# One launch for attention and routed experts: the opening drawn into the attention pipeline, and the output projection in plain fp32

## The chip, the cores and the metric

The kernel runs on one core of one Trainium2 chip. The metric is the device time of one execution in microseconds (us), as the median of several runs. The profile shown below is one further execution, taken by the hardware profiler.

## The reference, cut to what matters

```python
B, T, C = 4, 1024, 256          # 16 heads of 64; 32 experts, hidden 1024, 8 tokens for each expert
xn = layernorm(x)
# attention: causal, with rotary embedding
q, k, v = xn @ Wq, xn @ Wk, xn @ Wv                    # (B, T, 1024) each
q, k = rope(q), rope(k)
attn = softmax(where(causal, q @ k.T * 64**-0.5, -inf))
a = (attn @ v) @ Wo + bo
# experts: each expert picks its 8 tokens by a softmax over the tokens
probs = softmax(xn @ gate_w.T + gate_b, axis=tokens)
vals, idx = top_k(probs, 8)                            # for each batch and expert
merged = einsum(xn[idx], vals)                         # (B, 32, 256)
o = concat(gelu(concat(merged, 1) @ w1), 1) @ w2       # (B, 32, 256)
f = zeros.at[idx].add(o * vals)
out = x + a + f
```

All inputs and outputs are fp32.

## The kernel before

There are three blocks, one after the other, each with its own instruction lists for the five engines and a common barrier at its end (`build`).

`prepare_block` runs over the four batches: it loads x, normalises it (`normalise`), transposes it on TensorE, splits the transposed rows into a high half (rounded to fp32r) and a low half (the remainder), stores both in `xt_s`, and adds up the gate logits, 12 matmuls for each batch (L267). `route_block` makes the softmax over the tokens, picks the eight largest, stores the gates (`wsp_s`), merges the tokens of each expert (L379), splits Wo into halves and stores it (`wo_s`), and loads the rotation tables.

`attend_block` is a pipeline written out by hand. Its unit is a *pair*: two heads of one batch, 32 pairs in all (N = B x PAIRS), and a pair P has six *stages* (P, g), g = 0 to 5. The list STAGES gives the order in which every engine goes through its work, so an engine that has to wait holds back everything behind it in its list. In a stage, TensorE makes the scores of two chunks (`scores`, L1076 to L1088), the scores that give row maxima for the next pair (`maximum`, L1100 and L1106), one projection of a later pair (`fill`, L1130 for v, L1144 for q and k), and the products with v (`values`, L1169). ScalarE takes the exponentials (L818) and empties the projections (`evict`, L834 and L839), VectorE makes the maxima (L940), the rotation's first product and the low halves (L974, L964), GpSimd the rotation's second product and the sums of the exponentials, and SyncE issues most DMAs: the swapped rows of the rotation (`t_swap<-t_raw`, L743), the round trips through DRAM that spread the softmax sums (`store_sums`, `spread_recip`), and weights. For pairs below 8 the raw weights are loaded, split into halves (`weights_of`, L915 and L1049) and stored; later pairs load the halves.

Two kinds of work are hung into stages. *Slots* (`slots_of`) are the expert layers: for each of eight groups of four experts, four `layer1`, four `turn` and four `layer2` slots, in pairs -1 to 7; w1 and w2 (1 MB for each expert and layer) are loaded by ScalarE's queue. *Outputs* (`outputs_of`) are the 32 tiles of 128 rows of the result. A tile of batch y is computed in the first two pairs of batch y + 1; those of batch 3 stand behind the last pair. For each tile ScalarE rounds the attention's rows (`round_out`, L882), VectorE makes the remainder (`rest`, L1008), TensorE adds 24 matmuls with the three products of halves (L1218) and one fp32 matmul for the experts' part (L1221), and VectorE adds x and the bias (L1017). The product of the halves is this:

```python
for k in range(PAIRS):
    for o, hw in ((oh, 0), (oh, 1), (ol, 0)):
        pe.matmul(bank, o[:, t % 2, k, :], wo[:, hw, k, :], start=(a == 0), stop=False)
        a += 1
pe.wait_ge(moe_loaded, (y + 1) * 80)
pe.matmul(bank, wsp[:, t * P128:(t + 1) * P128], oe[:, :], start=False, stop=True)
```

The stages (-2, 0) to (-1, 5) fill the pipeline: projections of pairs 0 and 1, maxima of pair 0, and the first layer1 slots.

## Time and profile before

| | us |
|---|---|
| median of 3 runs (lowest, highest) | 1481.48 (1481.37, 1485.4) |
| the profiled execution, its own time | 1488.41 |
| span of the profile, first to last instruction | 1486.6 |
| granted TensorE clock, mean share over the span | 0.976 |

The span is cut below into stretches that start and end at the first exponential of a pair (L818): pair 0's is at 128.0 us, pair 1's at 176.9, pair 4's at 336.3, pair 5's at 384.2, pair 6's at 434.8, pair 7's at 492.2, pair 8's at 536.9, pair 10's at 636.8, pair 11's at 671.5, pair 13's at 740.8, pair 15's at 810.8, pair 16's at 845.8, pair 18's at 942.2. `prepare_block` ends at 60.5 us, `route_block` at 77.9 us, and the last eight tiles of the result begin at 1448.3 us. The clock column (PEclk) is the granted share of 2.4 GHz.

### The profile page before, as it was taken

To read this page: it belongs to the slowest core of one execution; us is meant where nothing else is said; L and a number is where in the kernel's file an instruction comes from. 1 tells how busy PE (TensorE), PEld (TensorE's weight loads), DVE (VectorE), ACT (ScalarE), POOL (GpSimd) and SP (SyncE) were. 2 spreads that over 40 slices of the span, in tenths; PEclk is the share of its full clock that TensorE was granted. 3 is DMA by queue.
4 is the path that set the end of the run, shared out by engine and by line. 5 is a ranking of instruction groups with operands and counts; after the bars stand their busy time and mean duration, and the time that the engine had idled before them with its cause. 6 is when DMAs were issued, how large, how long until landed. Compare 5 with 4: busy or idle time off the path is not lost.

```text
span 1486.6 us, 31037 instructions
## 1 busy us (share of the span) xinstructions
PE 1348.0 (91%) x11644; PEld 873.1 (59%) x11644; DVE 908.9 (61%) x1200; ACT 623.9 (42%) x919; POOL 990.1 (67%) x664
## 2 busy tenths in 40 slices
PE   3547988889898899999999999999999999999977
PEld 2424545545555467666666677666666776666646
DVE  7436656556565456666666765667666756666633
ACT  1214344424433433444544534444445444444541
POOL 1034556546555656788887866888878778888861
PEclk9779999999999899999999999999999999999999
DMA  5756757755776452212223222121232222212111
GB/s 201 273 196 219 250 174 237 252 181 190 261 265 210 142 161 79 76 62 76 75 88 108 84 76 76 58 72 66 80 115 80 90 81 68 76 59 73 45 48 57
DMA packets 112959, 188.85 MB, mean 127 GB/s; under 512 B 30064, under 2 KB 49936, under 8 KB 112432
## 3 DMA queue, kind: packets, MB, share of 16 engines
q1 hardware_dynamic: 85312, 115.39, 23.5%
q10 hardware_dynamic: 27456, 71.34, 14.2%
q8 instruction: 99, 1.62, 0.5%
q14 instruction: 44, 0.36, 0.1%
q0 software_dynamic: 48, 0.13, 0.0%
HBM read 130.58 MB, written 22.54 MB: 103 GB/s over the span
## 4 chain that ended last, share of the span: by engine, by line
PE 72%; DMA 9%; DVE 6%; issue 4%; ACT 2%; SPq 1%; POOL 0%; ACTq 0%; POOLq 0%
PE t_pO L1169 15%; PE t_pF L1144 11%; PE t_pA L1076 8%; PE t_pB L1076 6%; PE t_pF L1130 6%; DMA t_swap<-t_raw 6%; PE t_pC L1218 3%; PE t_pB L1218 3%; PE t_pA L1100 3%; PE t_pC L1100 3%; PE t_pA L1081 2%; PE t_pC L1178 2%; PE t_pB L1081 2%; DVE t_LO L964 1%; PE t_pC L1106 1%
## 5 line engine op out<-in xcount | busy, mean ns | idle before, releaser
L783 POOL TENSOR_TENSOR t_acc<-t_acc,t_PT 128x1024 f32<-128x1024 f32 (+3 forms) x256 | 435.9, 1703 | 146.5 <-ACT t_PT L818 126.7
L760 POOL TENSOR_TENSOR t_swap<-t_swap,s_sin 128x512 f32<-128x512 f32 x128 | 168.7, 1318 | 228.2 <-DMA t_swap<-t_raw 227.8
L1169 PE MATMUL t_pO<-t_PT,t_V 128*64 128x512 f32 (+3 forms) x1536 | 293.1, 503 | 4.4 <-ACT t_PT L818 4.4
L818 ACT ACTIVATE t_PT<-t_pA 128x1024 f32<-128x1024 f32 x192 | 169.7, 884 | 285.5 <-PE t_pA L1088 243.8
L1144 PE MATMUL t_pF<-t_xT,t_wqk 128*128 128x512 f32 x768 | 215.7, 417 | 19.9 <-DMA t_xT<-xt_s 11.9
L763 POOL TENSOR_TENSOR t_rot<-t_rot,t_swap 128x512 f32<-128x512 f32 x128 | 194.3, 1518 | 10.0
L964 DVE TENSOR_TENSOR t_LO<-t_rot,t_HI 128x512 fp32r<-128x512 f32 x128 | 150.1, 1172 | 82.2 <-ACT t_HI L849 82.0
L1169 PEld LDWEIGHTS t_pO<-t_PT,t_V 128*64 128x64 f32 x1536 | 93.7, 136 | 142.0 <-issue 118.7
L1144 PEld LDWEIGHTS t_pF<-t_xT,t_wqk 128*128 128x128 f32 x768 | 136.2, 190 | 62.4 <-issue 29.4
L940 DVE TENSOR_REDUCE s_nm<-t_pC 128x2 f32<-128x256 f32 (+2 forms) x96 | 71.7, 775 | 146.6 <-PE t_pC L1106 146.6
L839 ACT ACTIVATE t_raw<-t_pF 128x512 f32<-128x512 f32 x128 | 76.4, 597 | 194.8 <-PE t_pF L1144 143.7
L818 ACT ACTIVATE t_PT<-t_pB 128x768 f32<-128x768 f32 (+1 forms) x192 | 141.9, 739 | 6.3 <-PE t_pB L1081 4.4
L780 POOL TENSOR_TENSOR t_acc<-t_PT 128x768 f32<-128x768 f32 x64 | 139.5, 2180 | 7.1 <-ACT t_PT L818 7.1
L940 DVE TENSOR_REDUCE t_nma<-t_pC 128x2 f32<-128x1024 f32 x64 | 78.4, 1225 | 85.5 <-PE t_pC L1100 85.5
L974 DVE TENSOR_TENSOR t_rot<-t_pF,s_cos 128x512 f32<-128x512 f32 x128 | 87.3, 682 | 47.4 <-ACT t_raw L839 46.9
L932 DVE TENSOR_TENSOR t_OT<-t_OT,t_OC 128x512 f32<-128x512 f32 x64 | 106.6, 1666 | 11.1 <-DMA t_OT<-r_s 11.1
L1130 PE MATMUL t_pF<-t_wvs,t_xT 128*128 128x256 f32 x768 | 108.5, 291 | 0.0
L1130 PEld LDWEIGHTS t_pF<-t_wvs,t_xT 128*128 128x128 f32 x768 | 95.4, 190 | 11.3 <-issue 8.0
L1076 PE MATMUL t_pA<-t_HI 64*128 64x512 f32 (+1 forms) x384 | 89.1, 461 | 1.4 <-DVE t_nmb L940 1.4
L864 ACT ACTIVATE t_srow<-t_pC 128x256 f32<-128x256 f32 x64 | 24.6, 385 | 148.2 <-PE t_pC L1178 148.2
L1076 PEld LDWEIGHTS t_pA<-t_HI 64*128 64x128 f32 x384 | 35.9, 184 | 82.3 <-issue 79.7
L1081 PE MATMUL t_pA<-t_D,s_onesr 64*128 64x512 f32 (+1 forms) x384 | 70.2, 362 | 15.0 <-DVE t_D L954 14.7
(153 smaller groups left out, 2464.7 us busy)
## 6 DMA issues: line engine op xcount, KB each, us to landing
t_w1t<-in_L_ffn_w ACTq DMA_DIRECT2D x32, 1024.0 KB, 6.6
t_swap<-t_raw SPq DMA_DIRECT2D x256, 128.0 KB, 2.1
t_w2t<-in_L_ffn_w ACTq DMA_DIRECT2D x32, 1024.0 KB, 9.5
t_OT<-r_s SPq DMA_DIRECT2D x128, 128.0 KB, 3.0
t_wqk<-wqk_s SPq DMA_DIRECT2D x24, 512.0 KB, 4.2
xt_s<-a_xThl SPq DMA_DIRECT2D x16, 512.0 KB, 3.5
t_xT<-xt_s SPq DMA_DIRECT2D x8, 1024.0 KB, 8.2
t_wvs<-wv_s SPq DMA_DIRECT2D x12, 512.0 KB, 3.6
```

Of the source, the lines that this page charges most:

```text
L760: pool.tensor_tensor(swap[:, r % 2, :], swap[:, r % 2, :], sin[:, c * BANK:(c + 1) * BANK], ALU.mult).then_inc(sin_done, 1)
L763: pool.tensor_tensor(rot[:, r % 2, :], rot[:, r % 2, :], swap[:, r % 2, :], ALU.add).then_inc(rot_done, 1)
L780: pool.tensor_tensor(a[:, :, off:], first[:, :, off:], pt, ALU.add).then_inc(acc_done, 1)
L783: pool.tensor_tensor(a[:, :, off:], a[:, :, off:], pt, ALU.add).then_inc(acc_done, 1)
L818: act.activation(PT[:, n % PTS, :, 0:w], bank[:, :, 0:w], ACT.Exp, scale=SCALE).then_inc(exp_done, 1)
L940: op = dve.tensor_reduce(dst, bank[:, :, at:at + w], AX_X, ALU.max, negate=True)
L964: dve.tensor_tensor(LO[:, P % 2, z, q], rot[:, r % 2, :], HI[:, P % 2, z, q].bitcast(F32), ALU.subtract).then_inc(lo_done, 1)
L1076: pe.matmul(bank[:, h, 0:w], hk[d, P % 2, 1, k], hq[d, P % 2, 0, q], start=(a == 0), stop=False)
L1081: mm = pe.matmul(bank[:, h, 0:w], onesr[d, :], D[d, c, off // P128:, :].rearrange("p i q -> p (i q)"), start=False, stop=not diag)
L1130: mm = pe.matmul(pF[:, u * 2 * P128:(u + 1) * 2 * P128], xT[:, c, hx, k, q], wvs[:, hw, k, :], start=(a == 0), stop=(a == 3 * KT - 1))
L1144: mm = pe.matmul(pF[:, :], wqk[:, hw, k, z * P128:(z + 1) * P128], xT[:, c, hx, k, :], start=(a == 0), stop=(a == 3 * KT - 1))
L1169: mm = pe.matmul(pO[h * DH:(h + 1) * DH, off:], v, PT[:, n % PTS, h, 0:w], start=(j == 0), stop=(j == 4 * c + 3))
```

## The change

The three blocks become one. Only batch 0 is normalised and transposed ahead of the pipeline, in two halves of four tiles (`statistics(0)`, `statistics(1)`, `first_transposes`), straight from PSUM into `xT` (`first_high`, `first_low`), without the way through `xt_s`. Six projections, the rotations of pair 0 (in buffers of their own, `raw_of`, `swap_of`, `rot_of`) and four of its maxima are written out by hand; STAGES now begins at (-1, 4). TensorE issues 12 matmuls on the identity while it waits for x.

The rest of the old opening becomes 13 *units*, hung into stages of pairs 0 to 4 (`UNITS_AT`): six `x` units (transpose half a batch, split it, store it to `xt_s`), four `logit` units, `gates`, `merge` and `merged`. The statistics of batches 1 to 3 are in stages (0, 0) to (0, 2), their square roots in (0, 3), the normalising on ScalarE in six later stages (`NORM_AT`), the top-8 choice in (3, 3) and (3, 4). The expert slots start five pairs later (MOE = 5: pairs 4 to 12).

The output projection is eight fp32 matmuls for a tile in place of 24 with halves; `round_out`, `rest` and the stored halves of Wo go. Batch 0's tiles are computed in pairs 13 and 14; until then its attention rows are parked in DRAM (`o0_s`, stored by SyncE, 256 KB for each half pair) and come back, 512 KB for a tile, into two buffers (`os`). The tiles of batches 1 and 2 start one stage earlier, and `start_output` with them.

```diff
+MOE = 5
 def slots_of(P, g):
-    if P == -1:
-        return {2: [("layer1", 0, 0), ("layer1", 0, 1)], 3: [("layer1", 0, 2)]}.get(g, [])
+    G = P - MOE
+    if G == -1:
+        return [("layer1", 0, g - 3)] if g > 2 else []
 def outputs_of(P, g):
     y, p = divmod(P, PAIRS)
+    if MOE + E // GE <= P <= MOE + E // GE + 1:
+        n = (P - MOE - E // GE) * GROUPS + g - 1
+        return [(0, n)] if 0 <= n < NT else []
     if P == N:
         tiles = [(), (0, 1), (2,), (3,), (4, 5), (6, 7)][g]
     else:
-        tiles = {0: [(), (0, 1), (2,), (3,), (4,), (5,)], 1: [(6,), (7,), (), (), (), ()]}.get(p, [()] * GROUPS)[g]
-    return [(y - 1, t) for t in tiles] if y > 0 else []
+        tiles = {0: [(0,), (1,), (2,), (3,), (4,), (5,)], 1: [(6,), (7,), (), (), (), ()]}.get(p, [()] * GROUPS)[g]
+    return [(y - 1, t) for t in tiles] if y > 1 else []
+UNITS_AT = {(0, 5): ("logit", 0), (1, 1): ("x", 1, 0), (1, 3): ("x", 1, 1), (1, 5): ("logit", 1), (2, 0): ("x", 2, 0),
+            (2, 1): ("x", 2, 1), (2, 3): ("logit", 2), (2, 4): ("x", 3, 0), (2, 5): ("x", 3, 1), (3, 1): ("logit", 3),
+            (3, 5): ("gates",), (4, 0): ("merge",), (4, 1): ("merged",)}
+STATISTICS_AT = {(0, 0): 1, (0, 1): 2, (0, 2): 3}
+MOMENTS_AT = {(0, 4): 1, (0, 5): 2, (1, 0): 3}
+NORM_AT = {(0, 5): (1, 0), (1, 0): (1, 1), (1, 1): (2, 0), (1, 2): (2, 1), (1, 3): (3, 0), (1, 4): (3, 1)}
-STAGES = [(P, g) for P in PERIODS for g in range(GROUPS)]
+STAGES = [(-1, 4), (-1, 5)] + [(P, g) for P in range(N + 1) for g in range(GROUPS)]
+FIRST_FILLS = [("k", 0, 0), ("q", 0, 0), ("v", 0, 0), ("v", 0, 2), ("q", 0, 1), ("k", 0, 1)]
...
         @block.sync
+                n = normalise_of(*STAGES[s - 4]) if s >= 4 else None
+                if n is not None and n < 2 * PAIRS:
+                    sp.wait_ge(o_done, n + 1)
+                    sp.dma_start(o0_s[n // 2, :, n % 2 * BANK:(n % 2 + 1) * BANK],
+                                 OT[:, ot_slot(n // 2), n % 2 * BANK:(n % 2 + 1) * BANK]).then_inc(o0_stored, 16)
...
+                for y, t in next_outputs(s):
+                    if y == 0:
+                        if t >= 2:
+                            sp.wait_ge(y_mm, t - 1)
+                        sp.wait_ge(o0_stored, 2 * PAIRS * 16)
+                        sp.dma_start(os[:, t % 2, :, :], o0_s[:, :, t * P128:(t + 1) * P128].rearrange("p r t -> r p t")).then_inc(os_loaded[t % 2], 16)
...
         @block.vector
+            dve.wait_ge(g_trans, 1)
+            dve.wait_ge(g_zero, 1)
...
+            dve.wait_ge(x0_loaded[0], 16)
+            statistics(0)
+            moments(0)
...
+            weights_low(("qk", 0))
+            dve.wait_ge(x0_loaded[1], 16)
+            statistics(1)
+            first_low(0)
+            weights_low(("v", 0))
+            moments(1)
+            dve.wait_ge(table_loaded[0], 32)
+            rope(("k", 0, 0))
+            rope(("q", 0, 0))
+            first_low(1)
+            first_turn(("q", 0, 0))
+            dve.wait_ge(table_loaded[1], 32)
+            rope(("q", 0, 1))
+            low(("k", 0, 0))
+            low(("q", 0, 0))
+            first_maximum(0)
+            first_maximum(1)
+            rope(("k", 0, 1))
+            first_maximum(2)
+            first_turn(("q", 0, 1))
+            weights_low(("qk", 1))
+            low(("q", 0, 1))
+            first_maximum(3)
+            low(("k", 0, 1))
+            dve.wait_ge(g_hi, 1)
+            dve.tensor_tensor(gThl[:, 1, :, :, :], gT[:, :, :, :], gThl[:, 0, :, :, :].bitcast(F32), ALU.subtract).then_inc(g_lo, 1)
...
         @block.tensor   (output, and the unit among a stage's work)
-                pe.wait_ge(ol_done, n + 1)
                 pe.wait_ge(wo_loaded, 16)
-                a = 0
+                if y:
+                    pe.wait_ge(o_done, 2 * (y * PAIRS + PAIRS - 1) + t // 4 + 1)
+                else:
+                    pe.wait_ge(os_loaded[t % 2], (t // 2 + 1) * 16)
                 for k in range(PAIRS):
-                    for o, hw in ((oh, 0), (oh, 1), (ol, 0)):
-                        pe.matmul(bank, o[:, t % 2, k, :], wo[:, hw, k, :], start=(a == 0), stop=False)
-                        a += 1
+                    o = OT[:, k, t * P128:(t + 1) * P128] if y else os[:, t % 2, k, :]
+                    pe.matmul(bank, o, wot[:, k, :], start=(k == 0), stop=False)
...
+                if u:
+                    unit(u)
```

A unit writes the banks `pC[:, 1]` and `pB[:, 1]`. ScalarE and VectorE read them (`unit_read`), and the second score chunk and the next maxima of the stage behind wait for that.

## Rows read from the trace of the kernel before

**Rows 1.** The page: each engine's busy time, share of the span, instructions.

```profile
PE 1348.0 (91%) x11644; PEld 873.1 (59%) x11644; DVE 908.9 (61%) x1200; ACT 623.9 (42%) x919; POOL 990.1 (67%) x664
```

**Rows 2.** Stretches: from:to, us, each engine's busy time (instructions), PEclk, DMA share, GB/s.

```profile
0.00:60.50 60.50, 27.30 (x114) 21.14 (x114) 39.26 (x122) 10.88 (x14) 8.48 (x18) 0.94 0.63 226
60.50:77.90 17.40, 8.96 (x74) 4.66 (x74) 8.30 (x10) 5.46 (x5) 1.02 (x3) 0.61 0.60 226
77.90:128.00 50.10, 25.35 (x183) 16.95 (x183) 20.95 (x30) 8.83 (x15) 14.03 (x12) 0.80 0.76 266
128.00:384.20 256.20, 226.67 (x2150) 134.07 (x2152) 153.64 (x221) 105.57 (x152) 147.56 (x97) 0.97 0.64 211
336.30:384.20 47.90, 44.13 (x436) 26.44 (x434) 31.19 (x44) 21.00 (x30) 29.11 (x20) 1.00 0.68 225
384.20:434.80 50.60, 44.59 (x438) 26.68 (x437) 30.69 (x45) 21.50 (x32) 29.64 (x20) 1.00 0.69 227
434.80:492.20 57.40, 46.17 (x436) 27.38 (x436) 28.63 (x43) 20.41 (x30) 30.41 (x22) 0.94 0.67 231
492.20:536.90 44.70, 42.36 (x386) 26.16 (x384) 26.61 (x36) 20.51 (x29) 26.75 (x18) 0.96 0.42 132
536.90:636.80 99.90, 96.28 (x806) 69.60 (x808) 62.06 (x71) 41.63 (x60) 66.67 (x47) 1.00 0.31 97
636.80:671.50 34.70, 34.70 (x302) 21.91 (x302) 23.96 (x28) 16.95 (x27) 29.40 (x19) 1.00 0.19 63
740.80:810.80 70.00, 70.00 (x610) 44.25 (x608) 44.19 (x54) 33.65 (x53) 56.36 (x37) 1.00 0.30 98
845.80:942.20 96.40, 96.03 (x806) 69.27 (x806) 65.98 (x71) 41.55 (x61) 71.22 (x49) 1.00 0.25 80
1448.30:1484.00 35.70, 28.86 (x208) 26.81 (x208) 12.08 (x17) 6.35 (x6) 6.56 (x8) 0.96 0.18 57
```

**Rows 3.** Chain of waits, 78 to 128 us: start, us, what.

```profile
78.89 10.08 DMA t_xT<-xt_s
...
89.11 2.90 PE t_pF L1144 x6
...
109.68 5.05 DMA t_w1t<-in_L_ffn_w
...
114.87 1.07 PE t_pC L1193 x16
...
120.33 7.13 DMA t_swap<-t_raw
```

**Rows 4.** Timeline, 6 to 78 us: start, us, engine, line, operation, count, idle before.

```profile
6.56 2.71 DVE L200 BATCH_NORM_STATS2 a_stats<-a_xin 128x6 f32<-128x256 f32 x8 [6.56 <-DMA a_xin<-in_L_attn_x]
...
11.52 2.58 DVE L228 TENSOR_SCALAR s_xn<-a_xin,a_mean,a_rstd 128x256 f32<-128x256 f32 x7
...
31.44 1.91 PE L259 MATMUL a_pT<-s_ident,s_xn 128*128 128x128 f32 x16
...
36.08 3.07 PE L267 MATMUL a_pL<-a_xThl,a_gThl 128*128 128x512 f32 x12 [2.73 <-DVE a_xThl L240]
...
69.65 6.55 PE L379 MATMUL r_pM<-s_xn,r_WT 128*32 128x256 f32 x64 [1.11 <-ACT r_WT L343]
```

**Rows 5.** Chain of waits over the first of the last eight tiles.

```profile
1448.31 4.35 PE t_pC L1218 x24
1452.67 0.43 PE t_pC L1221 x2
1453.10 2.87 PE t_pB L1218 x24
...
1456.87 1.23 issue
```

**Rows 6.** Groups by form, weight loads: count, busy us, mean ns, idle before.

```profile
L1218 PEld LDWEIGHTS t_pB<-t_wo,t_oh 128*128 128x128 f32 x256 | 40.4, 191 | 2.9 <-issue 2.1
...
L1221 PEld LDWEIGHTS t_pB<-t_oe,t_wsp 128*128 128x128 f32 x32 | 5.0, 192 | 0.0
```

More of the change, by code:

```diff
@@ L596, in next_outputs, with fill_bank, unit_bank, units_before @@
             return outputs_of(*STAGES[s + 1]) if s + 1 < len(STAGES) else []
+        def fill_bank(f):
+            first = {("q", 0, 0): pO[:, :], ("k", 0, 1): pO[:, :], ("v", 0, 0): pC[:, 0, :], ("v", 0, 2): pC[:, 1, :]}
+            return first[f] if f in first else pF[:, :]
+        def unit_bank(u):
+            return (pC, pB)[u][:, 1, :]
+        def units_before(s):
+            return sum(t in UNITS_AT for t in STAGES[:s])
+        def doubles_before(s):
+            return sum(UNITS_AT.get(t) in DOUBLE for t in STAGES[:s])
+        def ot_slot(P):
+            return P % 2 if P < PAIRS else P % PAIRS
+        def turned(engine, r):
+            if r < EARLY:
+                engine.wait_ge(first_turned[r], 1)
+            else:
+                engine.wait_ge(rot_done, r - EARLY + 1)
         def slot_bank(n):
@@ L812, in exp @@
                 act.wait_ge(s_done, n + 1)
-                if n >= PTS:
+                if n < PTS:
+                    for r in range(2 * (n % 2), 2 * (n % 2) + 2):
+                        if n < 2:
+                            act.wait_ge(first_swapped[r], 32)
+                        else:
+                            act.wait_ge(first_turned[r], 1)
+                else:
                     m = n - PTS
@@ new lines, in choose @@
+            def choose():
+                for c in range(2):
+                    dve.wait_ge(unit_read[c], (DOUBLE if c else UNIT)["logit", 3] + 1)
+                dve.max(top[:, :], L[:, :]).then_inc(route_done, 1)
+                dve.wait_ge(route_done, 1)
+                dve.tensor_scalar(nmax[:, :], top[:, 0:1], -1.0, None, ALU.mult).then_inc(route_done, 1)
+                dve.wait_ge(xs_stored[0], (B - 1) * 16)
+                dve.wait_ge(xs_stored[1], (B - 1) * 16)
+                dve.match_replace(out=Lr[:, :], in_to_replace=top[:, :], in_values=L[:, :], imm_value=USED).then_inc(route_done, 1)
+                dve.wait_ge(route_done, 3)
+                dve.tensor_tensor(taken[:, :], Lr[:, :], L[:, :], ALU.not_equal).then_inc(route_done, 1)
@@ L1054, in _ @@
                         read_slot(*x_)
-                for y, t in next_outputs(s):
-                    rest(y, t)
         @block.tensor
@@ new lines, in _ @@
+            pe.wait_ge(ident_made, 2)
+            pe.wait_ge(g_loaded, 16)
+            for k in range(KT):
+                tr = pe.transpose(pC[:, 0, k * E:(k + 1) * E], gw[:, k * P128:(k + 1) * P128], ident[0:E, 0:E])
+            tr.then_inc(g_trans, 1)
+            for i in range(12):
+                pe.matmul(pO[:, 0:P128], ident[:, :], ident[:, :], start=True, stop=True)
+            first_transposes(0)
+            fill(("k", 0, 0))
+            fill(("q", 0, 0))
+            pe.wait_ge(g_copied, B)
@@ L1251, in _ @@
                     turn_maxima(P + 1, 0)
-                if banks and (slots or outputs_of(P, g) or normalise_of(P, g) is not None):
+                if banks and (u or slots or outputs_of(P, g) or normalise_of(P, g) is not None):
                     pe.wait_ge(max_done, MAXES[P, g] + 1)
+                if u:
+                    unit(u)
                 for x_ in slots:
```

934 lines of the change are left out of this document (515 added, 419 removed).

## The prediction, on record before the changed kernel ran

> **What bounds the kernel now.** I read the page first: TensorE is busy for 91% of the span, VectorE and GpSimd for about two thirds [rows 1]. An average over such different parts says little, so I cut the span at the first exponential of each pair and read the stretches [rows 2]. Three regimes show.
>
> A plain pair, with neither expert slots nor outputs, takes 34.7 us, and TensorE is busy in all of it. Outputs are added at the price of their matmuls: pairs 16 and 17 take 96.4 us, 27.0 more than 2 x 34.7, or 3.37 for each of eight tiles [rows 2]. There every microsecond of TensorE's work counts and nobody else's does.
>
> The pairs with expert slots take 47.9 us at best (pair 4), with TensorE busy for 44.1, and on average (256.2 + 50.6) / 6 = 51.1 over pairs 0 to 5; DMA engines are busy for 0.64 to 0.69 of that time against 0.19 in a plain pair [rows 2]. The slots' work is about 44.1 - 34.7 = 9.4 us; the rest is waits.
>
> Up to the first exponential, 128.0 us pass in which TensorE is busy for 27.3 + 9.0 + 25.4 = 61.7 us, partly at 1.2 GHz (shares of 0.61 and 0.80) [rows 2]. The chain of waits there shows what it waits for: 10.08 us for xT coming back from DRAM, 5.05 for w1, 7.13 for the rotation's swapped rows, which queue behind the expert weights [rows 3]. None of the three blocks overlaps the next. This is where the change can win.
>
> **The change part by part.** *(a) The opening, 128.0 us now.* VectorE sets its pace in the new order. Its statistics can start at about 6.5 us: x for eight tiles lands at 6.56 now [rows 4], half of it will be there sooner, but the gate copies ahead of them wait for their own load. Four tiles of statistics take 2.71 / 2 = 1.4, the small steps up to the first normalised tile 2.2 (9.3 to 11.5), two tiles of normalising 0.9 [rows 4]: 11.0 us. Then, in its list, a weight remainder (0.7, an estimate), the second half's statistics (2.3) and two remainders of x (1.4 together, an estimate too): TensorE's first projection starts at about 15.5 us, where it starts at 89.1 now [rows 3].
>
> From there to the first exponential it is 38.9 us now. Two of its waits belong to the expert weights, which no longer load here: 38.9 - 7.1 - 5.0 = 26.8; three slots leave it too, at 1.07 each [rows 3], so 23.6. New in it are the second half of x (its transposes and remainders, 3.5) and the gate weights' remainder (1.2), which makes 28.3. So the first exponential comes at 44 us by that, and at 15.5 + 38.9 = 54.5 if the waits are only replaced, say by the swapped rows of four rotations and by VectorE, which is busy for 20.95 us of today's stretch and has all of that and more in one hand-written line [rows 2]. I take 48: **-80.0 us** (bounds -84 and -73).
>
> *(b) Pairs 0 to 4, 256.2 us now* [rows 2]. The expert slots go to pairs 5 to 12, except three layer1 slots in pair 4 (3.2 us). The floor is TensorE's work: 5 x 34.7 = 173.5, 3.2, and the units. These are four logit units at 3.07 (12.3), six x units at half of 1.91 (5.7), gates 1.0, the merge 3.3 (6.55 now, in a stretch at a clock of 0.61, so about half), and 0.3 for the last transposes [rows 2, 4]: 22.6 us. Floor: 199.3.
>
> The cover is thin in places. An x unit's banks are released only after two ScalarE copies and two VectorE remainders, about 2.5 to 4 us after its transposes, and TensorE has the v products and one score chunk, some 2.5 to 3.5 us, ahead of that wait. The statistics put about 3.6 us of VectorE's work into each of three stages of some 5.8 us, in which it is busy for two thirds already (23.96 of 34.7) [rows 2]; the square roots need two table loads on ScalarE; the top-8 choice puts some 4 us, half of the 8.30 that VectorE is busy in `route_block`, into one stage [rows 2], and the gates in the next wait for ScalarE's exponential. Behind VectorE stand the maxima, and TensorE waits for them. I add 12 units x 0.7, 3 x 1.5 and 4 for the choice, together 17. The upper bound keeps all of today's waits: 256.2 - 5 x 9.4 + 25.8 = 235. I take 216, nearer the floor, because the long waits of today hang on transfers that leave: **-40.2 us** (bounds -57 and -21).
>
> *(c) Pairs 5 to 12, which get the expert slots.* Now they take 50.6 + 57.4 + 44.7 + 99.9 + 3 x 34.7 = 356.7 us [rows 2]. Pairs 5 and 6 keep what they have (108.0). Pairs 7 to 11 become full expert pairs. Against pair 4 they no longer have the halves of new weights to make, but they load 512 KB of stored halves, and up to pair 8 SyncE stores the parked attention rows, each behind a wait for VectorE's multiplication with the swapped rows of the rotation queued behind it. I take 49 each, between 47.9 and 51.1. Pair 12 is like pair 7 now, 44.7. The sum is 397.7: **+41.0 us** (bounds: 47.9 each, +35; 53 each, +61).
>
> *(d) Batch 0's eight tiles in pairs 13 and 14.* An fp32 matmul of this shape, 256 columns behind a new 128x128 weight, is the experts' one: 0.43 us on the chain [rows 5]. A tile becomes 9 x 0.43 = 3.87 us where it is 3.37. The two pairs take 70.0 us [rows 2]; with 8 x 3.87 = 31.0 and the 3.5 us by which pairs 8 and 9 exceed pairs 16 and 17 (start of the outputs: stores, waits, loads one after the other in SyncE's list) it is 104.5: **+34.5 us**. The tiles' return from DRAM is issued a stage ahead, some 9 us before it is needed by my count of the stages. No row is such a load; at the opening's 226 GB/s [rows 2] 512 KB take 2.3 us, and I double that for the short pieces. I count nothing, and 2.5 us a tile as the bound (+20).
>
> *(e) Batches 1 and 2.* Sixteen tiles at 0.5 more, with a half microsecond for each batch: **+9.0 us**. The rounding on ScalarE and the remainder on VectorE lay beside TensorE's work, since these stretches are TensorE's alone; their going gives nothing here.
>
> *(f) The last eight tiles.* Here the remainder is on the path: after two tiles at 4.35 (partly cold) and 2.87, each plus 0.43, the chain waits 1.23 us and more before the next. The stretch is 35.7 us [rows 2, 5]. Eight tiles at 3.87 are 31.0, with 0.7 for the cold start 31.7: **-4.0 us**.
>
> The sum is -80.0 - 40.2 + 41.0 + 34.5 + 9.0 - 4.0 = -39.7 us. The span of the profiled execution goes from 1486.6 to 1446.9, its own time from 1488.4 to 1448.7; that execution stands 6.9 us above the median of the runs, so the forecast for the median is 1481.5 - 39.7 = **1442 us**.
>
> **The rivals.** *A: the gain is given back in pairs 0 to 4.* The units and statistics wait on VectorE stage after stage, and the opening only replaces its waits: 235 and 54.5, or 1442 + 19 + 6.5 = 1467 us. For it speaks that TensorE's slack between unit and next score chunk is about nil; against it, that VectorE is free for 10 us of a plain pair.
>
> *B: the waits vanish with the weights.* Pairs 0 to 4 at 203, the opening at 44, the expert pairs at 48: 1442 - 13 - 4 - 5 = 1420 us. For it, TensorE's 34.7 of 34.7 in plain pairs.
>
> *C, the other side: the fp32 matmuls do not hide their weight loads.* There are 256 of them. If each of the two passes over a weight waited for its load, a matmul would cost 2 x (0.191 + 0.213) = 0.81 us by the load's row and half of 0.43, and the time would be 1442 + 256 x 0.38 = 1539 us. It decides from 0.43 + 39.7 / 256 = 0.585 us a matmul. Against it: the experts' fp32 matmul loads its weight twice within its 0.43 us, and its loads last as long as those of the fp32r ones, 192 and 191 ns [rows 5, 6]. For it: the trace has no eight in a row with such weights. The Trainium skill (TensorE: Matmul & The Clock Gate, Weight-path perf modes — Fast Weight Load (FWL) and DoubleRow) says that the fast weight load is off for fp32, and gives 107 ns for a load of 128 columns; fully exposed, an estimate by that page is 0.64 us a matmul, and the time 1496. The rows show no difference between the two kinds of load, so they do not bear it out.
>
> *D: the parked rows come back late.* At the bound of (d), 1442 + 20 = 1462 us.
>
> **How the numbers follow.** My forecast has 0.54, A 0.15, B 0.14, D 0.08, C 0.07, and A with D together, about 1485, 0.02. The likeliest one's own range is 1426 to 1457. The range 1414 to 1470 takes in A, B and D and leaves out C, A with D, and the far tails of the rest. Within 0.3%, about 4.4 us, is what a measurement of this kernel can tell from no change. Faster: 0.91; same: 0.02; slower: 0.07.
>
> **What would show it.** In the trace after: the first exponential at 48 us, and the first projection at 15 to 16; pair 5's first exponential at 264, pair 13's at 662; plain pairs still at 34.7; a tile's eight fp32 matmuls at 3.4 to 3.5 us; 31 to 32 us for the last eight tiles. It would go wrong if pairs 0 to 4 show TensorE waiting for VectorE or ScalarE behind units, if the swapped rows still take 7 us in the opening, if the expert pairs pass 51 us once they share the queue with stored weights and parked rows, or if an fp32 matmul takes more than 0.45 us.

## The result, and the profile after

The changed kernel takes 1469.97 us (median of 6 runs, 1467.65 to 1475.1) against 1481.42 us beside it: ratio 0.9923, 95% interval 0.9899 to 0.9947. It is faster by 11.5 us (0.8%, clear of noise), where 39.5 were forecast. The mechanism is there, but less than a third of the gain arrives. The profiled execution took 1472.21 us (span 1470.3), 2.2 above its median; that of the kernel before lay 6.9 above its own. So 4.7 us of the 28.0 that are missing are the distance of two profiled executions from their medians, and 23.4 stand in the spans. The time lies at the very end of the forecast's range (1414 to 1470) and outside the likeliest one's (1426 to 1457).

The page of the changed kernel, the lines that answer to [rows 1]:

```profile
PE 1366.1 (93%) x11412; PEld 887.6 (60%) x11412; DVE 865.1 (59%) x1169; ACT 615.3 (42%) x937; POOL 961.0 (65%) x662
```

Its stretches, columns as in [rows 2]: the opening, pairs 0 to 4, pair 0, pair 2, pairs 5 and 6, pairs 5 to 12, pairs 13 and 14, pairs 16 and 17, and the last eight tiles.

```profile
0.00:50.60 50.60, 31.36 (x177) 23.77 (x177) 32.82 (x74) 19.09 (x32) 14.52 (x31) 0.87 0.56 182
50.60:276.10 225.50, 204.36 (x1686) 133.09 (x1686) 159.10 (x230) 116.48 (x189) 143.73 (x95) 0.96 0.37 129
50.60:99.80 49.20, 40.20 (x302) 26.56 (x302) 41.02 (x83) 23.41 (x38) 31.11 (x22) 0.93 0.17 60
141.90:183.60 41.70, 41.36 (x342) 27.77 (x340) 28.64 (x36) 23.05 (x37) 28.16 (x19) 1.00 0.33 115
276.10:328.90 52.80, 45.98 (x438) 27.67 (x440) 31.79 (x47) 21.60 (x32) 32.40 (x22) 0.97 0.61 206
328.90:390.90 62.00, 47.52 (x436) 28.75 (x434) 30.10 (x43) 20.42 (x30) 30.05 (x22) 0.90 0.63 221
276.10:679.90 403.80, 357.67 (x3426) 217.35 (x3428) 232.52 (x341) 165.17 (x234) 233.27 (x154) 0.97 0.64 216
679.90:787.50 107.60, 103.44 (x755) 72.40 (x752) 47.62 (x61) 33.56 (x52) 61.53 (x45) 0.98 0.42 128
822.80:923.20 100.40, 100.40 (x744) 70.56 (x744) 50.57 (x62) 33.81 (x53) 65.18 (x48) 1.00 0.21 67
1435.30:1467.70 32.40, 32.34 (x146) 27.85 (x144) 3.79 (x10) 0.38 (x1) 4.60 (x7) 0.97 0.20 62
```

Set against the terms of the prediction (before from [rows 2], all in us of the span):

| term | forecast | measured | missing |
|---|---|---|---|
| (a) opening | -80.0 | 50.6 - 128.0 = -77.4 | 2.6 |
| (b) pairs 0 to 4 | -40.2 | 225.5 - 256.2 = -30.7 | 9.5 |
| (c) pairs 5 to 12 | +41.0 | 403.8 - 356.7 = +47.1 | 6.1 |
| (d) pairs 13 and 14 | +34.5 | 107.6 - 70.0 = +37.6 | 3.1 |
| (e) batches 1 and 2 | +9.0 | 4.0 + 4.3 = +8.3 | -0.7 |
| (f) last eight tiles | -4.0 | 32.4 - 35.7 = -3.3 | 0.7 |
| everything else | 0 | +2.1 | 2.1 |
| span | -39.7 | -16.3 | 23.4 |

The third row is the one to look at: in pair 0 VectorE is busy for 41.0 of 49.2 us and TensorE for 40.2, while in pair 2, which has five units, TensorE is busy for 41.4 of 41.7. The units of pair 2 hide; the statistics of pair 0, which has one unit, do not.

The chain of waits through pair 0 lies on VectorE. From its third stage (of six; a stage is two exponentials):

```profile
69.44 1.80 DVE t_nm L942 x3
...
72.43 2.63 DVE t_stats L1018 x8
...
75.46 2.25 DVE t_mean L1025
...
77.90 2.30 DVE t_ve L1029
80.20 1.13 DVE t_nm L942
```

`t_mean` is a step on 128x8 elements. The timeline of VectorE there, and of GpSimd below it, shows why it lasts 2.25 us and its neighbours 0.16:

```profile
75.26 0.17 DVE L1023 TENSOR_TENSOR t_square<-t_stats 128x8 f32<-128x8 f32 x1
75.46 2.25 DVE L1025 TENSOR_SCALAR t_mean<-t_both 128x8 f32<-128x8 f32 x1
77.63 0.15 DVE L1026 TENSOR_TENSOR t_gap<-t_gap 128x8 f32<-128x8 f32 x1
77.71 0.16 DVE L1027 TENSOR_SCALAR t_mse<-t_square 128x8 f32<-128x8 f32 x1
77.90 2.30 DVE L1029 SCALAR_TENSOR_TENSOR t_ve<-t_gap,t_mse 128x8 f32<-128x8 f32 x1
...
66.30 2.37 POOL L672 TENSOR_TENSOR t_acc<-t_PT 128x1024 f32<-128x1024 f32 x1
75.25 4.93 POOL L675 TENSOR_TENSOR t_acc<-t_acc,t_PT 128x1024 f32<-128x1024 f32 x2 [6.58 <-ACT t_PT L746]
```

Two accumulations of 2.46 us run from 75.25 to 80.18. `t_mean` ends at 77.71, where the first one does, and `t_ve` at 80.20, where the second does; between the two, small steps pass at 0.15 and 0.16. A step that starts within 0.01 us of the first one (L1023) isn't held. The eight `bn_stats` of a batch (2.63 on the chain, in the first two sets beside GpSimd's work as in the third without it) and the maxima from PSUM (1.21 each) keep their durations. Each set of statistics took 5.6, 5.25 and 7.8 us of the chain (56.8, 64.2 and 72.4 to the end of `t_ve`), together 18.6, where I had counted 3 x 3.6 = 10.8.

Pair 3 has the choice. Its chain holds `t_LO` 1.65 and `t_OT` 2.79 beside GpSimd, then the choice itself (`t_top`, `t_Lr` and `t_taken`, which is issued at 215.45 and lasts 2.72), 5.2 us together, before the maxima that TensorE waits for:

```profile
208.44 1.65 DVE t_LO L966
210.09 2.79 DVE t_OT L934
212.88 1.15 DVE t_top L1071
...
214.13 1.30 DVE t_Lr L1076 x2
```

Pair 4 waits for small transfers behind 4 MB of first expert weights, issued in its second and fourth stages:

```profile
240.52 7.04 DMA t_comp<-s_s
...
253.18 2.83 DMA s_s<-t_srow
256.02 7.47 DMA t_comp<-s_s
...
263.75 3.97 DMA r_s<-t_rcomp
...
270.10 4.17 DMA t_swap<-t_raw
```

Pair 6 waits twice for swapped rows of 128 KB, and pair 13 for the first parked rows, which SyncE issues only after a store has landed and nine other issues have gone:

```profile
333.33 10.91 DMA t_swap<-t_raw
...
370.54 13.71 DMA t_swap<-t_raw
...
680.29 2.03 DMA o_s<-t_part
...
682.37 0.31 SPq L513
...
684.10 1.58 SPq L514
...
686.73 0.47 SPq L613
687.24 0.60 SPq L613
687.88 4.14 DMA t_os<-o_s
```

The last eight tiles go as forecast, eight fp32 matmuls (x16: the trace has two passes of each) in 3.45 us and no wait between the tiles:

```profile
1435.31 4.62 PE t_pC L1363 x16
1439.93 0.43 PE t_pC L1365 x2
1440.37 3.45 PE t_pB L1363 x16
1443.82 0.43 PE t_pB L1365 x2
1444.25 3.45 PE t_pC L1363 x16
```

### The profile page after: what moved, and what is told of

Its sections match the earlier page's. It is cut to its first block, busy times and chain, and to the rows that moved or that the text cites. A ratio compares the mean times of both kernels' runs of the same rounds, so it can differ in the third digit from the quotient of the medians.

```text
span 1470.3 us, 30876 instructions
## 1 busy us (share of the span) xinstructions
PE 1366.1 (93%) x11412; PEld 887.6 (60%) x11412; DVE 865.1 (59%) x1169; ACT 615.3 (42%) x937; POOL 961.0 (65%) x662
## 4 chain that ended last, share of the span: by engine, by line
PE 73%; DVE 10%; DMA 8%; issue 4%; ACT 3%; SPq 1%; POOL 0%; ACTq 0%; POOLq 0%; DVEq 0%
PE t_pO L1312 14%; PE t_pF L1287 11%; PE t_pA L1210 8%; PE t_pB L1210 6%; DMA t_swap<-t_raw 5%; PE t_pF L1270 5%; PE t_pC L1363 4%; PE t_pB L1363 4%; PE t_pA L1234 3%; PE t_pC L1234 2%; PE t_pA L1215 2%; PE t_pC L1321 2%; DVE t_LO L966 2%; PE t_pB L1215 2%; DVE t_OT L934 1%
## 5 line engine op out<-in xcount | busy, mean ns | idle before, releaser
L650 POOL TENSOR_TENSOR t_swap<-t_swap,t_sin 128x512 f32<-128x512 f32 x124 | 162.2, 1308 | 238.2 <-DMA t_swap<-t_raw 237.8
L746 ACT ACTIVATE t_PT<-t_pA 128x1024 f32<-128x1024 f32 x192 | 169.5, 883 | 305.9 <-PE t_pA L1222 265.5
L966 DVE TENSOR_TENSOR t_LO<-t_rot,t_HI 128x512 fp32r<-128x512 f32 x124 | 157.0, 1266 | 83.6 <-ACT t_HI L778 83.6
L653 POOL TENSOR_TENSOR t_rot<-t_rot,t_swap 128x512 f32<-128x512 f32 x124 | 174.6, 1408 | 9.7
L942 DVE TENSOR_REDUCE t_nm<-t_pC 128x2 f32<-128x256 f32 (+2 forms) x96 | 71.5, 773 | 135.8 <-PE t_pC L1240 135.8
L672 POOL TENSOR_TENSOR t_acc<-t_PT 128x768 f32<-128x768 f32 x64 | 139.9, 2187 | 17.0 <-ACT t_PT L746 16.9
L746 ACT ACTIVATE t_PT<-t_pB 128x768 f32<-128x768 f32 (+1 forms) x192 | 141.7, 738 | 9.2 <-PE t_pB L1222 8.3
L934 DVE TENSOR_TENSOR t_OT<-t_OT,t_OC 128x512 f32<-128x512 f32 x64 | 100.7, 1574 | 14.2 <-DMA t_OT<-r_s 14.2
L976 DVE TENSOR_TENSOR t_rot<-t_pF,t_cos 128x512 f32<-128x512 f32 x124 | 84.7, 683 | 37.3 <-ACT t_raw L768 36.8
L1210 PE MATMUL t_pA<-t_HI 64*128 64x512 f32 (+1 forms) x384 | 89.3, 462 | 8.8 <-DVE t_nma L942 7.4
L1234 PE MATMUL t_pA<-t_HI 64*128 64x512 f32 (+1 forms) x320 | 76.1, 469 | 17.8 <-ACT t_PT L746 12.5
## 6 DMA issues: line engine op xcount, KB each, us to landing
t_swap<-t_raw SPq DMA_DIRECT2D x248, 128.0 KB, 2.1
t_OT<-r_s SPq DMA_DIRECT2D x128, 128.0 KB, 3.0
```

What stands on the lines that cost most here:

```text
L650: pool.tensor_tensor(swap_of(r), swap_of(r), sin[:, c * BANK:(c + 1) * BANK], ALU.mult).then_inc(sin_sem, 1)
L653: pool.tensor_tensor(rot_of(r), rot_of(r), swap_of(r), ALU.add).then_inc(rot_sem, 1)
L672: pool.tensor_tensor(a[:, :, off:], first[:, :, off:], pt, ALU.add).then_inc(acc_done, 1)
L746: act.activation(PT[:, n % PTS, :, 0:w], bank[:, :, 0:w], ACT.Exp, scale=SCALE).then_inc(exp_done, 1)
L942: op = dve.tensor_reduce(dst, bank[:, :, at:at + w], AX_X, ALU.max, negate=True)
L966: dve.tensor_tensor(LO[:, P % 2, z, q], rot_of(r), HI[:, P % 2, z, q].bitcast(F32), ALU.subtract).then_inc(lo_done, 1)
```

## The experiments

Pair lengths below are taken between first exponentials (L746 of the changed kernel), one profile for each kernel. How far they can be trusted is seen in the kernels whose edit leaves a pair alone: there pair 0 lasts 47.7 to 50.7 us, pair 3 44.5 to 46.5, pair 4 45.7 to 49.5, pair 5 50.7 to 54.8, pair 6 59.1 to 64.4 and pair 13 57.5 to 60.7. An effect is read as shown where it leaves this spread, and its size is good to a few microseconds. Medians of one kernel differ by up to 3 us between two sets of runs. Of the single edits only two, the small steps once and the choice spread, have an interval of the ratio that lies clear of the changed kernel's 0.9899 to 0.9947; for the others the pair lengths alone decide.

| us | median | ratio | first exp. | pair 0 | 3 | 4 | 5 | 6 | 13 |
|---|---|---|---|---|---|---|---|---|---|
| changed | 1470.0 | 0.992 | 50.6 | 49.2 | 45.7 | 46.8 | 52.7 | 62.0 | 59.6 |
| control | 1473.0 | 0.995 | 51.8 | 49.1 | 46.1 | 47.0 | 54.4 | 63.0 | 60.1 |
| small steps on GpSimd | 1470.6 | 0.993 | 50.5 | 49.1 | 46.0 | 49.1 | 54.8 | 63.7 | 60.0 |
| short accumulations | 1468.4 | 0.991 | 50.5 | 44.4 | 46.5 | 49.5 | 50.7 | 63.0 | 59.8 |
| small steps once | 1459.8 | 0.986 | 51.9 | 43.4 | 45.7 | 46.8 | 50.9 | 63.1 | 59.7 |
| choice spread | 1461.5 | 0.987 | 51.5 | 47.7 | 40.5 | 47.0 | 53.7 | 64.0 | 57.5 |
| expert loads spaced | 1466.3 | 0.990 | 50.7 | 49.6 | 45.9 | 42.1 | 55.3 | 61.7 | 60.2 |
| tile inputs early | 1464.9 | 0.988 | 50.4 | 50.7 | 44.5 | 45.7 | 53.9 | 59.1 | 55.5 |
| nothing parked | 1465.2 | 0.987 | 50.3 | 49.5 | 45.8 | 47.1 | 49.4 | 62.7 | 59.5 |
| xT load small | 1465.7 | 0.988 | 52.7 | 47.8 | 46.5 | 46.4 | 52.7 | 56.2 | 59.9 |
| gate weights first | 1472.1 | 0.992 | 51.5 | 48.1 | 45.7 | 47.5 | 53.0 | 61.6 | 60.7 |
| together | 1452.5 | 0.979 | 49.2 | 45.0 | 40.7 | 43.3 | 52.3 | 64.4 | 56.7 |

**Control.** The changed kernel, unedited.

> The changed kernel itself once more, as the control for the kernels beside it. Its pair 0 (from the first exponential of pair 0 to that of pair 1) lasted 49.2 us, pair 3 45.7, pair 4 46.8, pair 6 62.0, pair 13 59.6 in its first profile. If these excesses come from fixed collisions of the schedule, they come back within 1 us and the time lies within 0.3% of 1470; if they are accidents of one execution, they move by several us.

1472.99 us, ratio 0.995 (0.9927 to 0.9972). Pairs 0, 3, 4, 6 and 13 come back within 0.1 to 1.1 us. So the excesses of pairs 0, 3, 4 and 13 belong to the schedule, not to one execution; for pair 6 see below.

**The output projection alone**, in the kernel before.

```diff
-        wo = sb("t_wo", [P128, 2, PAIRS, C], F32R)
-        oh = sb("t_oh", [P128, 2, PAIRS, P128], F32R)
-        ol = sb("t_ol", [P128, 2, PAIRS, P128], F32R)
+        wot = sb("t_wot", [P128, PAIRS, C])
...
                 for k in range(PAIRS):
-                    for o, hw in ((oh, 0), (oh, 1), (ol, 0)):
-                        pe.matmul(bank, o[:, t % 2, k, :], wo[:, hw, k, :], start=(a == 0), stop=False)
-                        a += 1
+                    pe.matmul(bank, OT[:, k, t * P128:(t + 1) * P128], wot[:, k, :], start=(k == 0), stop=False)
```

> The kernel before with the output projection in fp32 alone (no halves, no buffers for batch 0's tiles beyond what it had). My theory (the size of terms d to f of the prediction): two output periods per batch grow by some 4 us each batch against before, the last eight tiles lose about 4, so 1481 + 8 = 1489 (1484 to 1494). It follows that the opening and the units are worth about 20 us net of what they push into later pairs, not the 32 forecast. Rival: the output projection is where the missed gain lies, and this kernel loses 15 us or more (1496 up). Second rival: fp32 saves VectorE and ScalarE work enough to be faster, 1478 or less.

1490.9 us, ratio 1.0071 (1.0045 to 1.0096), as expected. Pair 16 lasts 58.0 us, pair 17 42.4, exactly as in the changed kernel, and 55.1 and 41.3 before. The last eight tiles take 33.2 us here, 32.4 in the changed kernel, 35.7 before. So the size of terms (e) and (f) was right, and all the rest of the change (the opening with its units, net of what it pushes into later pairs) is worth 18 to 21 us: 1490.9 against 1470.0 to 1473.0.

**The small steps on GpSimd.** Batches 1 to 3 only, behind the accumulations in program order; the steps are as they were, but for the last, which VectorE does in one instruction and GpSimd in two.

```diff
                 st.then_inc(done, 1)
+                if n > 1:
+                    return
...
                 for c, j in chunks_of(P, g):
                     accumulate(P, c, j)
+                if s and STAGES[s - 1] in STATISTICS_AT:
+                    small_steps(STATISTICS_AT[STAGES[s - 1]] + 1)
```

> The changed kernel with the five small steps of each of the statistics of batches 1 to 3 (sums, gap, mean, mse, variance, 128x8) on the engine that runs the accumulations, behind them in program order, not on VectorE beside them. My theory: in pair 0 a small VectorE step of 0.17 us lasts until the GpSimd operation beside it ends (1.1 to 2.3 us each), 15 us of VectorE in all; moved, pair 0 falls from 49 to 42 us and the kernel by 7 (1463). Rival 1: the volume of the statistics themselves (24 sums of 0.4 us, and the square roots with their table loads on ScalarE) sets pair 0; then it stays at 49 and the time at 1470. Rival 2: GpSimd is now late with its accumulations and pair 0 becomes longer, 1473.

Pair 0 stays at 49.1 us and the time at 1470.6 (0.9932, 0.9908 to 0.9956): my number missed. The stages tell more. The first three fall from 5.8 + 7.8 + 10.0 = 23.6 us to 5.8 + 4.2 + 7.3 = 17.3, and the next two rise from 10.7 + 6.2 = 16.9 to 14.7 + 8.5 = 23.2. The last set now stands behind two accumulations, and ScalarE waits for it with the square roots, and with the exponentials behind them:

```profile
76.67 2.34 POOL t_acc L693
79.00 0.17 POOL t_both L650
...
80.65 0.21 POOL t_ve L660
...
80.88 0.04 ACT t_sd L827
...
82.40 1.03 ACT t_PT L766
```

So VectorE is relieved, and GpSimd becomes the chain. This doesn't yet separate my theory from a second limit; the next two do.

**Short accumulations.** The sums of pair 0 are incomplete here.

```diff
                 off, w = chunk_span(c, j)
+                if P == 0 and j > 1:
+                    w = 16
...
-                    pool.tensor_tensor(a[:, :, off:], a[:, :, off:], pt, ALU.add).then_inc(acc_done, 1)
+                    pool.tensor_tensor(a[:, :, off:off + w], a[:, :, off:off + w], pt, ALU.add).then_inc(acc_done, 1)
```

> The changed kernel with GpSimd's accumulations of pair 0 (from the third block of each row chunk on) cut to 16 columns, so that the sums of pair 0 are incomplete; nothing else differs, and VectorE's own list is the same. My theory: a VectorE operation on SBUF that runs beside a GpSimd tensor_tensor ends only with it, so small steps of 0.17 us last 1.1 to 2.3; without the long accumulations the three sets of small steps go from 3.0, 2.6 and 5.1 us to about 1.1 each (some stay beside the rotations), and pair 0 from 49.1 to 43 to 45 us. After the run with the small steps on GpSimd the rival is: pair 0 has a second limit behind this one (the square roots and their table loads, the 24 sums of statistics), and stays at 48 or more even so.

Pair 0 falls to 44.4 us with VectorE's list untouched. The timeline of a step of the second set, and of the third set, in which `t_mean` and `t_ve` took 2.25 and 2.30:

```profile
66.34 2.36 DVE L1029 TENSOR_SCALAR t_mse<-t_square 128x8 f32<-128x8 f32 x1
...
74.93 0.17 DVE L1027 TENSOR_SCALAR t_mean<-t_both 128x8 f32<-128x8 f32 x1
...
75.28 0.17 DVE L1031 SCALAR_TENSOR_TENSOR t_ve<-t_gap,t_mse 128x8 f32<-128x8 f32 x1
```

The third set's small steps take 0.8 us, not 5.1. The cause is shown: take the long GpSimd operation away, and the same VectorE instruction lasts 0.17 us. My 1.1 us for each set was too low for the other two. The first takes 2.1 and still runs beside a rotation of 1.3. The second takes 3.0, more than its 2.6 before: its `t_mse` lasts 2.36 and ends at 68.70, beside the one long accumulation that the edit leaves in (66.26 to 68.67). The three sets together fall from 10.7 to 5.9 us, by as much as the pair. The time moved by only 2 to 5 us (1468.4), of which the medians can't tell more.

**The small steps once**, on 128x24 elements, in the third stage.

```diff
+                if 1 < n < B:
+                    st.then_inc(done, 4)
+                    return
+                if n == B:
+                    b, c = slice(1, B), slice(0, NT)
                 st.then_inc(done, 1)
...
-                act.wait_ge(stat_done[n], 4)
+                act.wait_ge(stat_done[B if n > 1 else n], 4)
```

> The changed kernel with the small steps of the three statistics done once for all three batches (128x24 elements) in the third stage of pair 0, not three times. Moving them to GpSimd shortened the first three stages from 23.6 to 17.3 us and gave the same 6.3 back in the fourth, where the square roots waited for the third set behind GpSimd's accumulations. My theory: here two of three sets (5.6 us) go from VectorE, the third comes no later, and pair 0 falls to 44 us, the time by 5. Rival: the gain of the first two stages is again given back where the square roots and their table loads stand, pair 0 at 48 to 49.

Pair 0 falls to 43.4 us, by 5.7 against the control, and the time to 1459.8 (0.9858, 0.9826 to 0.989). The rival is out. The time falls by 10 to 13 us, twice what was expected and twice what pair 0 gives; in the profiles the rest stands mostly in pairs 5 and 7 (3.5 and 2.9 us under the control), which this edit doesn't touch, so it is not explained. The floor of this pair, 34.7 and one logit unit (3.07, [rows 4]), is 37.8, so 5.6 us remain.

**The choice spread** over three stages of pair 3.

```diff
-                if (P, g) == (3, 3):
+                if (P, g) == (3, 2):
                     choose()
+                if (P, g) == (3, 3):
+                    choose_more()
                 if (P, g) == (3, 4):
                     weigh()
```

(`choose_more` is the replacement of the eight maxima; the comparison that made `t_taken`, 2.72 us beside GpSimd, goes to `weigh`, and ScalarE's exponential is asked for a stage sooner.)

> The changed kernel with the steps of the top-8 choice on VectorE spread over three stages of pair 3 (maximum and first steps one stage sooner, the rest where they are, the last comparison with the gates). My theory: pair 3, whose fifth stage lasts 10.4 us where the same stage of pair 2 lasts 6.7, falls from 46 to 43 us. Rival: what lengthens that stage is the gates' wait for ScalarE's exponential and its table loads, not the choice's 4 us; then pair 3 stays at 46.

Pair 3 falls from 46 to 40.5 us, its fifth stage from 10.6 to 5.9; the time is 1461.5 (0.9866, 0.9835 to 0.9896), again more (8.5 to 11.5 us) than the pair. The rival said that the wait for the exponential sets the stage. Since the edit also asks for the exponential sooner, it doesn't separate the two cleanly; the chain of the changed kernel, which holds the choice on VectorE and no wait for ScalarE there, speaks for the choice.

**The first expert loads spaced.**

```diff
                     load_w1(0)
+                if (P, g) == (MOE - 1, 2):
                     load_w1(1)
-                if (P, g) == (MOE - 1, 3):
+                if (P, g) == (MOE - 1, 5):
                     load_w2(0)
+                if (P, g) == (MOE, 0):
                     load_w2(1)
```

> The changed kernel with the first two loads of w1 and of w2 (4 MB) at four stages, not two (the second w1 one stage later, the first w2 two later, the second w2 in pair 5). My theory: in pair 4 the small transfers of the sums' reciprocals wait 7 us behind this burst, and pair 4 is 5 us over its floor; spaced, pair 4 falls from 46.8 to about 43 and the time by 3 to 4 (1466). Rival: the burst only moves into pair 5 and the sum of pairs 4 to 6 (161.5 us) stays within 1.5 us, time 1470. Worse: the first w2 comes too late for the first expert's second layer and pair 5 grows, 1474.

Pair 4 falls from 47 to 42.1 us, more than expected, and pair 5 rises by 0.9 to 2.6, so that 2 to 4 us of it are left. 1466.3 us (0.9901, 0.987 to 0.9932). No `t_comp` transfer stands in pair 4's chain of waits any more; its two take 3.4 us in the median, not 7.3.

**Tile inputs early.** In `start_output`, batch 0 leaves out the gate weights and the inputs x of its first two tiles; they are loaded in pair 12.

```diff
+                if (P, g) == (MOE + E // GE - 1, 3):
+                    sp.wait_ge(wsp_stored, 16)
+                    for j in range(4):
+                        sp.dma_start(wsp[j * E:(j + 1) * E, :], wsp_s[0, :, :]).then_inc(moe_loaded, 16)
+                if (P, g) == (MOE + E // GE - 1, 4):
+                    for t in range(2):
+                        load_x(0, t)
```

> The changed kernel with the weights of the gates and the inputs of batch 0's first two tiles loaded in pair 12, not in SyncE's list at the start of pair 13. In pair 13 the second stage lasts 14 us (8.1 in pair 16), because 4 + 1 + 2 issues and two rotations stand ahead of the first parked rows. My theory: the parked rows come 2.5 to 3 us sooner and pair 13 falls from 59.8 to 57. Rival: the first parked rows wait for their own transfer (4.1 us) and the swapped rows as before; pair 13 stays within 0.5 us.

Pair 13 falls from 59.6 to 55.5 us, its second stage from 13.6 to 9.5, where pair 16 has 8.1. 1464.9 us (0.9877, 0.9844 to 0.991). The gain is 4.1 to 4.6, over the 3 expected, though pair 13 was 57.5 in the kernel with the choice spread, which has this part as it was. What is left of the chain there is the swapped rows' two issues and the parked rows' own transfer:

```profile
682.50 0.48 SPq L613
683.03 1.24 SPq L613
684.32 3.91 DMA t_os<-o_s
```

**Nothing parked.** Batch 0's output is not computed: the tiles' loads read a part of Wo.

```diff
-                if n is not None and n < 2 * PAIRS:
+                if n is not None and n < 0:
...
-                        sp.wait_ge(o0_stored, 2 * PAIRS * 16)
-                        sp.dma_start(os[:, t % 2, :, :], o0_s[:, :, t * P128:(t + 1) * P128].rearrange("p r t -> r p t")).then_inc(os_loaded[t % 2], 16)
+                        sp.dma_start(os[:, t % 2, :, :], wo[:, 0:P128].rearrange("(p r) t -> r p t", p=PAIRS)).then_inc(os_loaded[t % 2], 16)
```

> The changed kernel without the stores of batch 0's attention rows to DRAM; the loads for the output tiles read a part of Wo of the same size, so batch 0's output is not computed. It prices the parking. My theory: the misses of pairs 5 and 6 against what they took in the kernel before (52.7 to 54.4 against 50.6, 62 to 63 against 57.4) are these 256 KB stores, each with SyncE's wait for VectorE ahead of the swapped rows: pair 5 goes to 51 and pair 6 to 58, the time falls by 6 or 7. Rival: they come from the expert weights and the stored halves alone, and pairs 5 and 6 stay within 1 us; then the parking is as free as the prediction took it.

(Two other waits for the stores become waits for VectorE's multiplication.) Half right. Pair 5 falls to 49.4 us (50.6 before, [rows 2]), 3.3 and 5 us under the changed kernel and the control. But pair 5 was 50.7 and 50.9 in two kernels that park as before, so the parking is borne out as its excess, by 1.3 us at least, and its price isn't settled. Pair 6 stays at 62.7, so its excess over 57.4 is not the parking; the swapped rows there still take 9.78 and 12.68 us. The time is 1465.2, 5 to 8 us under the changed kernel's two medians.

**The xT load of pair 6 cut** to 64 KB of its 1 MB; batch 1's values are not computed rightly.

```diff
+                if (b, c) == (1, 1):
+                    sp.dma_start(xT[:, c, 0, 0, 0:128].bitcast(F32), xt_s[b, :, 0, 0, c * BANK:c * BANK + 128]).then_inc(xt_loaded[c], 16)
+                    return
```

> The changed kernel with batch 1's second half of the transposed input (1 MB, issued in the fifth stage of pair 6) cut to 64 KB, so that batch 1's values are not computed rightly. In that pair the swapped rows (128 KB) take 13.7 us behind it and behind w1 and w2, and the sixth stage lasts 16.4 us where the same stage of pair 5 lasts 8 to 9. My theory: the swapped rows wait for this one transfer; pair 6 falls from 62.5 to 55. Rival: w1 and w2 (2 MB of them in that stretch) hold them back by themselves, and pair 6 stays above 60.

Pair 6 falls to 56.2 us, its sixth stage from 16.7 to 9.2, and the swapped rows that took 13.71 take 8.12. The theory holds, but it explains a cost that was there before as well: in the kernel before the same transfer takes 12.45 us in pair 6 and the stage 15.4. The 5 us that the change adds to pair 6 stand mostly in its second and third stages (7.9 + 8.8 before, 10.5 + 9.5 after), behind the other half of xT, whose swapped rows go from 8.33 to 10.91 us. A part of that varies from one execution to the next: with the tile inputs early, an edit of pairs 12 and 13, pair 6 took 59.1 us, its second stage 6.4, and these rows came sooner:

```profile
334.27 6.83 DMA t_swap<-t_raw
```

**Gate weights first.**

```diff
+            act.dma_start(gw[:, :], gate_w).then_inc(g_loaded, 16)
             for n, w in enumerate((wq, wk)):
...
-            act.dma_start(gw[:, :], gate_w).then_inc(g_loaded, 16)
```

> The changed kernel with the router's weights issued ahead of Wq and Wk on ScalarE's queue. In the opening VectorE's gate copies wait for them until 7.45 us and the statistics behind them start at 8.6, where the prediction had 6.5. My theory: the load lands a microsecond sooner, the statistics start at 7.5 and the first exponential comes 1 us sooner, 49.6. Rival: Wq and Wk land that much later and nothing is gained (50.6), or the load takes its 5.6 us wherever it stands.

The statistics start at 5.0 us, sooner than expected, but ScalarE's first square root waits behind its copy of Wk, which lands at 7.59. The first projection starts at 15.89 us, not 17.20, but the first exponential comes at 51.5, and the time is 1472.1 (0.9919, 0.9892 to 0.9946). The lead is lost at the other end of the opening, where the last swapped rows take 4.57 us, against 2.99. With the same opening the next kernel has 2.60 there, and its first exponential comes at 49.2. Over all kernels with the changed opening the first exponential lies between 50.3 and 52.7, so a microsecond can't be told here.

**Together**: small steps once, choice spread, loads spaced, tile inputs early, gate weights first.

> The changed kernel with what the single runs bore out, together: the small steps of the statistics once for three batches (5.7 us of pair 0), the choice over three stages (5.4 of pair 3), the first expert loads spaced (4.9 of pair 4), gate weights and inputs of the first output tiles in pair 12 (4.3 of pair 13), and in the opening the router's weights loaded ahead of Wq and Wk. If these are separate terms, as my sums hold, they add to 20.3 us and about 1 for the opening: 1450 us against 1471 (1446 to 1455), and the ratio to before is 0.979. Rival: they share one cause behind them (the DMA queues, VectorE), and half is given back in pairs 5 and 6, 1460.

1452.46 us, ratio 0.9793 (0.9768 to 0.9817): faster than before by 2.1% (1.8 to 2.3), and than the changed kernel's two medians by 17.5 and 20.5. Its pairs 0 to 4 against 225.5:

```profile
49.20:262.10 212.90, 200.01 (x1688) 129.29 (x1686) 152.31 (x217) 116.56 (x190) 147.30 (x97) 0.98 0.37 129
```

The terms nearly add. Pairs 0, 3, 4 and 13 give 4.1, 5.4, 3.7 and 3.4 us against the control, of the 5.7, 5.6, 4.9 and 4.6 that they gave alone, and pair 6 takes 1.4 back. This holds for the pair lengths; the medians of the four single kernels are 13.2, 11.5, 6.7 and 8.1 us under the control's, together 39.5, of which 20.5 arrive, so they say little of each edit's own price.

## Why the prediction was wrong

**(a) The opening: right, 2.6 us short.** The statistics start at 8.63 us, not 6.5: the gate copies wait for `t_gw` until 7.45. I had written that they wait for their own load, and then left that wait out of the number. The first projection at 17.2 (15.5 forecast) carries 1.7 of it on, and from there to the first exponential it is 33.4 us, where 32.5 were forecast. The 7.13 us of the swapped rows [rows 3] are 2.99 here, so most of that wait left with the expert weights, as the step had it.

**(b) Pairs 0 to 4: the step that failed most.** "I add 12 units x 0.7, 3 x 1.5 and 4 for the choice, together 17." The sum was to be 17 and is 225.5 - 199.3 = 26.2, and it was put together wrongly. By pairs, over their floors, it is 11.4, 2.4, 0.1, 6.9 and 5.3. The x and logit units, half of my 17, cost next to nothing where most of them are: pair 2, with one logit unit and four x units, lasts 41.7, and its floor is 34.7 + 3.07 + 4 x 0.96 = 41.6. The 2.4 of pair 1 (three units and the last square root) are open. The statistics cost 49.2 - 37.8 = 11.4, not 4.5: about 5 of it (4.8 and 5.7 in two runs) are small steps that wait for GpSimd (shown by short accumulations and by small steps once), and the rest is open. Spreading the choice gave 5.2 to 5.6 back, more than the 4 that I had for it: operations ahead of it and within it are held up too. GpSimd accumulates from 207.16 to 217.08 there, four times 2.48; `t_taken`, issued at 215.45, lasts 2.72 and ends 1.1 after that, about its own length (1.21 when spread). And the burst of first expert weights in pair 4, about 5 us there, was no term at all: I had written the long waits off because "the long waits of today hang on transfers that leave", but the first of them (w1 and w2 of the first experts) are now issued in pair 4, still within this stretch.

The Trainium skill (SBUF — State Buffer, Who interferes with whom) states the rule: a VectorE instruction with two SBUF inputs contends with a GpSimd instruction that reads SBUF, and one in a two-port mode with GpSimd altogether; the one that issues first has the shared pair of ports for its whole length, and the other is blocked. The traces agree: the lengthened steps read SBUF alone and finish with GpSimd's instruction or just behind it (2.25 and 2.30 us against 0.17), and those that read PSUM, and `bn_stats`, keep their time. Which mode `t_mean`, a step with one input, ran in, no row shows. The prediction priced a small step at its duration in the old opening, where GpSimd was nearly idle (8.48 us busy of 60.5, [rows 2]). That was the mistake of reading: a row's duration holds for what ran beside it.

**(c) Pairs 5 to 12: the mechanism right, 6.1 short.** Pairs 7 to 11 were put at 49 each and took 49.7, 48.9, 48.9, 49.3 and 49.0; pair 12 took 43.3 for 44.7. The step that failed is "Pairs 5 and 6 keep what they have (108.0)": they took 52.8 + 62.0 = 114.8. In pair 5 it is in part the parking, which I had named for pairs 7 and 8 and not for these (49.4 without it, 50.7 to 54.8 with it). In pair 6 it is not; the cause of its 5 us is open, and 59.1 in one profile says that it is not all fixed by the schedule.

**(d) Pairs 13 and 14: 3.1 short.** The tiles themselves are right: pair 16, with six tiles, is 58.0. "I count nothing" for the return of the parked rows was the step: their load is asked for a stage ahead in program order, but SyncE's list has a wait for a store to land and nine issues before it, two of them a rotation's, so it goes out at 687.88 and lands at 692.0. Loading the inputs earlier gave 4.1 to 4.6 back, more than the 3.1, so it reached into the 3.5 that I had allowed for the start of the outputs.

**(e), (f) and the price of an fp32 matmul: right.** 3.45 us for eight, 0.43 each, with new weights every time. Rival C is out; it needed 0.585. The prediction's 0.64 is an estimate that takes every weight load as exposed, at the 107 ns for 128 columns that follow from the formula of the Trainium skill (TensorE: Matmul & The Clock Gate, LDWEIGHTS (loading the stationary operand)); the section that the prediction names has no such figure. The traces don't bear the estimate out: a matmul takes 0.43, and the loads of these weights, 190 ns each, lie within that.

**Everything else: 2.1.** Pairs 22 and 23 took 36.3 and 36.4 us in this profile and 35.7 and 35.1 in the control, so most of it belongs to one execution.

Of the rivals, A came nearest (1467), in part by luck: its price for pairs 0 to 4 was 235, for the opening 54.5, and both are too high, but its mechanism, VectorE's steps on TensorE's path, is the one that acts, in two of the five pairs. What it priced too high makes up for what (c), (d) and the distance between profile and median add, for which it had nothing. D, the parked rows late at 20 us, did not come: (d) is off by 3.1 in all. B's prices, 203 and 44, were not reached even by the kernel with all edits (212.9 and 49.2).

## What to carry to other kernels

Price a VectorE step by what GpSimd does beside it, not by its size: here a chain of small steps on SBUF waited once for each GpSimd instruction, so make one chain of several, or put it where GpSimd is idle. When work is moved under a dense pipeline, look for lumps (several microseconds in one stage of VectorE's list, 4 MB in two stages of a queue) rather than sums; spread over three stages, the same work cost 5 us less. And for each load that is "issued a stage ahead", count the issues and waits that stand before it in its queue's program order.
